# A perceiver block in one kernel: the end of attention, the first and the last group of the state-space stage in a new order

## The reference, cut to what matters

```python
x = x + xattn(layernorm(x), ctx)   # 32 query heads, 8 key/value heads of 128, RMS norm on q and k, 1601 keys
x = x + ssm(layernorm(x))          # 64 heads of 64 channels, state of 128, 8 groups
x = x + ffn(layernorm(x))          # the best of 8 experts per token, each of rank 16

# ssm, L = 64 steps:
proj = h @ in_proj.T               # gate (4096), x B C (4096 + 1024 + 1024), dt (64)
xBC  = silu(conv4(xBC) + bias)     # causal, 4 taps per channel
dt   = softplus(dt + dt_bias);  dA = exp(-exp(A_log) * dt)
state = state * dA_t + dt_t * x_t * B_t;   y_t = state @ C_t + x_t * D
y = y * rsqrt(mean(y * y over the 512 channels of a group) + eps) * norm_w * silu(gate)
out = y @ out_proj.T
```

## Time and profile before

| | us |
|---|---|
| runs | 2316.62, 2317.11, 2319.35 |
| profiled execution | 2317.6 |
| its span, from first to last instruction | 2315.2 |
| TensorE busy | 2273.6 (98%) |
| VectorE busy | 1917.5 (83%) |
| GpSimd busy | 1569.4 (68%) |
| ScalarE busy | 1300.2 (56%) |

### The profile page before, as it was taken

The page is one execution under the profiler, slowest core; times in us unless marked ns, Lnnn a source line. Parts: engine busy times, 40 slices in busy tenths (PEclk is TensorE's granted clock), DMA queues, the critical chain, the costliest instruction groups (busy, mean ns, idle before and its releaser), DMA issues. The chain is left out here.

```text
span 2315.2 us, 46570 instructions
## 1 busy us (share of the span) xinstructions
PE 2273.6 (98%) x19300; PEld 1645.4 (71%) x19300; DVE 1917.5 (83%) x2600; ACT 1300.2 (56%) x2090; POOL 1569.4 (68%) x1059
## 2 busy tenths in 40 slices
PE   8999999999999999999999999999999899999997
PEld 4577777778777778777878777877777544455554
DVE  7868888888888888888888888888888967888887
ACT  7854555545555545555545555555555446767763
POOL 0148888888888888888888788888888601433432
PEclk9999999999999999999999999999999999999999
DMA  8421000100000011000000000010001363212210
GB/s 293 128 56 35 26 19 27 29 26 27 27 27 23 29 28 33 18 27 29 27 27 27 27 22 29 27 35 10 10 29 32 112 214 110 83 65 83 92 46 19
DMA packets 101166, 117.54 MB, mean 51 GB/s; under 512 B 8286, under 2 KB 70878, under 8 KB 100958
## 3 DMA queue, kind: packets, MB, share of 16 engines
q1 hardware_dynamic: 98942, 107.25, 14.6%
q0 software_dynamic: 2016, 7.34, 1.2%
HBM read 96.74 MB, written 17.83 MB: 49 GB/s over the span
## 5 line engine op out<-in xcount | busy, mean ns | idle before, releaser
L178 POOL TENSOR_TENSOR p_l<-S,p_h 128x1792 f16<-128x1792 f32 x126 | 423.7, 3363 | 201.8 <-ACT p_h L489 201.8
L590 DVE SCALAR_TENSOR_TENSOR S<-pS,rk,mask 128x256 f32<-128x256 f32 x832 | 355.1, 477 | 130.4 <-PE pS L265 84.0
L265 PE MATMUL p_acc<-w_h,ctx_h 128*128 128x256 f16 (+1 forms) x1664 | 453.5, 273 | 2.3 <-DVE k_l L565 2.3
L265 PE MATMUL p_acc<-w_h,ctx_l 128*128 128x256 f16 (+1 forms) x1664 | 453.6, 273 | 0.0
L265 PE MATMUL p_acc<-w_l,ctx_h 128*128 128x256 f16 (+1 forms) x1664 | 453.6, 273 | 0.0
L600 DVE TENSOR_REDUCE mx<-S 128x256 f32<-128x3328 f32 x63 | 376.9, 5982 | 2.2
L265 PE MATMUL p_acc<-ctx_h,w_h 128*128 128x400 f16 x1016 | 337.6, 332 | 0.9 <-PEq L929 0.9
L265 PE MATMUL p_acc<-ctx_l,w_h 128*128 128x400 f16 x1016 | 337.6, 332 | 0.0
L471 ACT ACTIVATE v_h<-p_acc 128x512 f16<-128x512 f32 (+1 forms) x224 | 126.8, 566 | 374.2 <-PE p_acc L265 374.2
L265 PE MATMUL p_acc<-ctx_h,w_l 128*128 128x400 f16 x1016 | 336.9, 332 | 0.0
L637 DVE TENSOR_TENSOR S<-S,pO 128x1792 f32<-128x1792 f32 (+1 forms) x128 | 240.8, 1882 | 86.2 <-PE pO L335 86.2
(11 more groups left out here) (303 smaller groups left out, 5210.7 us busy)
## 6 DMA issues: line engine op xcount, KB each, us to landing
ctx_p<-ctxT_dram SPq DMA_DIRECT2D x42, 458.0 KB, 3.5
s_wst<-winG_dram SPq DMA_DIRECT2D x8, 1536.0 KB, 7.2
q_wst<-wqT_dram SPq DMA_DIRECT2D x8, 1024.0 KB, 6.4
o_scratch<-o_st SPq DMA_DIRECT2D x32, 256.0 KB, 2.4
s_wst<-winG_dram SPq DMA_DIRECT2D x8, 1024.0 KB, 5.3
m_wost<-woutG_dram SPq DMA_DIRECT2D x8, 1024.0 KB, 5.3
qh<-q_hi_scratch SPq DMA_DIRECT2D x64, 64.0 KB, 1.9
ql<-q_lo_scratch SPq DMA_DIRECT2D x64, 64.0 KB, 2.0
```

What stands on the lines that cost most here:

```text
L178: eng.tensor_tensor(p_l[:, s % 2, t0:t1, :], S[:, s % 2, t0:t1, :], p_h[:, s % 2, t0:t1, :], ALU.subtract).then_inc(pl_ok, 1)
L265: mm = pe.matmul(out, x, y, start=first and j == 0, stop=final and j == 2)
L590: ins = dve.scalar_tensor_tensor(out=S[:, s % 2, t, :].rearrange("p (r q) -> p r q", r=REP), in0=bank[:, t % 2, :].rearrange("p (r q) -> p ...
```

## The change

1. *Last unit of attention.* VectorE no longer folds: `first_maxima` is one reduce over key tiles 0 to 7, put after `output` and evacuation 5, with its output in the free half of bank `pO[1]`; `last_maxima` is a reduce over tiles 8 to 12 after evacuation 6 and a join. The tiles of projection step 1 are spread around the turns. Unit 62's sums over key tiles are no longer made by GpSimd's `total`; TensorE makes them from `p_h` and `p_l` with 26 products on ones. Step 2's low parts move from VectorE to GpSimd (ScalarE scales the stage for it); `high(4)` comes before the exponentials, `low(4)` before the last low parts.
2. *Banks of chunks.* From group 1 on, chunk n goes to `pI[(n + 1) % 3]`; output tile 1 goes to `pI[2]`. Group 1's chunks 0, 1, 2 each wait for the taps of group 0's chunks 7, 8, 9.
3. *Start.* Group 0's first `decay` comes after chunk 6, not 5. ScalarE gets a one-element Silu (`gate_table`) after `exponentials(1, 0)` in `second`, and after `exponentials(7, 1)` in `last`.
4. *Last group.* New queues on four engines. Decays 0 and 1 stand before chunks 5 and 6; the output tiles of group 6 come after all chunks, two of them in halves; the four key products lie side by side in `pI[0]`; each output tile has a bank that is free by then; `split_C` is in two parts on VectorE.

```diff
+        def in_bank(g, n):
+            return pI[(n + min(g, 1)) % 3]
         def keys_bank(g, t):
-            return pO[:, t * P:(t + 1) * P] if g == 0 else pCB
+            return pO[:, t * P:(t + 1) * P] if g == 0 else pI[0][:, t * P:(t + 1) * P] if g == L else pCB
+        def sum_bank(g, t):
+            if g == L:
+                return (pI[1], pO, pI[2], pI[0])[t]
+            return pI[2] if t == 1 or g == L - 1 and t == 3 else pO
...
+            def direct_denominators(s):
+                for t in range(KT):
+                    for part in (p_h, p_l):
+                        mm = pe.matmul(pO[s % 2][:, 1, :], ones_h[:, :], part[:, s % 2, t, :],
+                                       start=t == 0 and part is p_h, stop=t == KT - 1 and part is p_l)
+                mm.then_inc(den_ok, 1)
...
 # TensorE, last unit of attention and after it
+                        out_proj.multiply(pe, 1, (0,))
                         turn_maxima(b, s)
-                        out_proj.multiply(pe, 1, (0,))
+                        out_proj.multiply(pe, 1, (1,))
                     spread_maxima(b, s)
...
-            out_proj.multiply(pe, 1, (1, 2, 3))
-            denominators(NB - 1, U - 2)
+            direct_denominators(U - 2)
+            out_proj.multiply(pe, 1, (2, 3))
             out_proj.multiply(pe, 2, range(TT))
             for h in range(2):
                 values(NB - 1, U - 1, h)
-            out_proj.multiply(pe, 3, (0, 1))
-            denominators(NB - 1, U - 1)
-            out_proj.multiply(pe, 3, (2, 3))
+            out_proj.multiply(pe, 3, (0,))
+            denominators(NB - 1, U - 1, 1)
+            out_proj.multiply(pe, 3, (1, 2, 3))
 # VectorE, the same
             def first_maxima(s):
+                dve.wait_ge(o_ok, 2 * (U * NB - 2))
+                dve.wait_ge(s_out, 7 * (U * NB - 1) + 4)
+                dve.tensor_reduce(pO[s % 2][:, 0, :], S[:, s % 2, 0:8, :].rearrange("p t q -> p q t"), AX.X, ALU.max).then_inc(folded, 1)
+            def last_maxima(s):
...
+                dve.tensor_reduce(rest, S[:, s % 2, 8:KT, :].rearrange("p t q -> p q t"), AX.X, ALU.max).then_inc(folded, 1)
+                dve.wait_ge(folded, 2)
+                dve.tensor_tensor(mx[:, :], pO[s % 2][:, 0, :], rest, ALU.max).then_inc(mx_ok, 1)
...
             subtract(NB - 1, U - 1, 1)
-            output(NB - 1, U - 2)
-            dve.wait_ge(sum_ok, 5 * (U * NB - 1))
-            for h in range(2):
-                low(dve, NB - 1, U - 1, h)
-            total(dve, NB - 1, U - 1)
-            output(NB - 1, U - 1)
             dve.wait_ge(out_proj.lo, 8)
             out_proj.low(dve, 4)
+            low(dve, NB - 1, U - 1, 0)
+            output(NB - 1, U - 2)
+            low(dve, NB - 1, U - 1, 1)
+            total(dve, NB - 1, U - 1, 1)
+            output(NB - 1, U - 1)
...
 # input_chunk: waits
                 if n == 0:
                     wait(pe, wB_lo, g + 1)
-                    wait(pe, conv, CONV * g)
+                if n < 3:
+                    wait(pe, conv, CONV * g + (n - 2 if g == 1 else 0))
...
+            def gate_table():
+                act.activation(warm[:, :], eps[:, 0:1], ACT.Silu)
...
 # TensorE, last(g): from chunk 4 on
                 input_chunk(g, 4)
+                decay(g, 0)
                 outputs(g - 1, 3)
                 input_chunk(g, 5)
+                decay(g, 1)
+                for n in range(6, NIN):
+                    input_chunk(g, n)
+                squares(g - 1, 2)
+                squares(g - 1, 3)
+                turn_x(g, 0)
                 out_tile(g - 1, 1 - par, 0)
+                turn_x(g, 1)
+                out_tile(g - 1, 1 - par, 1, (0, 1))
+                for t in range(TT):
+                    keys_by_queries(g, t)
+                out_tile(g - 1, 1 - par, 1, (2, 3))
+                decay(g, 2)
+                outputs(g, 0)
+                out_tile(g - 1, 1 - par, 2)
+                turn_x(g, 2)
+                outputs(g, 1)
+                out_tile(g - 1, 1 - par, 3, (0, 1))
+                decay(g, 3)
+                out_tile(g - 1, 1 - par, 3, (2, 3))
+                turn_x(g, 3)
+                outputs(g, 2)
+                squares(g, 0)
+                out_tile(g, par, 0)
+                outputs(g, 3)
+                squares(g, 1)
+                out_tile(g, par, 1)
+                squares(g, 2)
+                out_tile(g, par, 2)
                 turn_normed(0)
                 squares(g, 3)
+                out_tile(g, par, 3)
                 logits(0)
-                out_tile(g, par, 3, out_bank[3])
 # VectorE, last(g): from taps 4 on
                 mean_square(g - 1)
+                times_dt(g, 0)
+                taps(g, 5)
                 accumulate(g - 1, 0)
+                times_dt(g, 1)
+                split_C(g, par, (0, 1))
+                causal(g, 0); causal(g, 1); masked(g, 0); masked(g, 1)
+                accumulate(g - 1, 1)
+                causal(g, 2); causal(g, 3); skip_added(g, 0); gated(g, par, 0); masked(g, 2)
+                accumulate(g - 1, 2)
+                times_dt(g, 2); skip_added(g, 1); gated(g, par, 1)
+                split_C(g, par, (2, 3))
+                masked(g, 3); times_dt(g, 3)
+                accumulate(g - 1, 3)
+                skip_added(g, 2); gated(g, par, 2); tile_mean_square(g, 0)
+                skip_added(g, 3); gated(g, par, 3)
                 accumulate(g, 0)
```

More of the change, by code:

```diff
@@ L550, in _ @@
             high(NB - 1, U - 1, 1)
-            for g in (4, 5, 6):
+            for g in (5, 6):
                 out_proj.high(act, g)
@@ L704, in body @@
                     evacuate(b, s, 3)
-                    if not ahead:
-                        first_maxima(s)
                     if before(b, s, 2):
@@ L723, in body @@
                     overall(b, s)
-                    if not ahead:
-                        out_proj.low_weights(dve, 2)
                     if s < NP and not last:
@@ L783, in body @@
                     squares(3)
-                    if earlier:
+                    if earlier and ahead:
                         total(pool, *earlier)
             loop(pool, body)
+            out_proj.low_of_scaled(pool, 2)
             out_proj.low_of_scaled(pool, 3)
@@ L1784, in outputs @@
                 wait(pe, yev, n)
-                wait(pe, cm, begun["cb"] if g else 0)
+                wait(pe, cm, begun["cb"] if 0 < g < L else 0)
                 wait(pe, msn, begun["ms"])
@@ L2145, in second @@
                 exponentials(1, 0)
+                gate_table()
                 finish_conv(1, 0)
@@ L2211, in last @@
                 first_tap(g, 0)
+                exponentials(g, 0)
                 square(g - 1, 3)
                 first_tap(g, 1)
+                exponentials(g, 1)
+                gate_table()
                 finish_conv(g, 0)
+                first_tap(g, 2)
                 high(g - 1, 3)
-                first_tap(g, 2)
                 finish_conv(g, 1)
@@ L2222, in last @@
                 first_tap(g, 5)
-                exponentials(g, 0)
                 finish_conv(g, 4)
+                split_C(g, par)
                 finish_conv(g, 5)
-                exponentials(g, 1)
+                exponentials(g, 2)
+                high(g, 0)
                 square(g, 0)
-                split_C(g, par)
-                high(g, 0)
-                exponentials(g, 2)
                 exponentials(g, 3)
@@ L2344, in causal @@
                 n = TT * g + t
-                wait(dve, cb, n + 1 if g else TT)
+                wait(dve, cb, n + 1 if 0 < g < L else TT * (g + 1))
                 wait(dve, m_ok, n - 1)
```

174 lines of the change are left out of this document (70 added, 104 removed).

## The result

Six runs of the changed kernel took 2301.75 to 2306.26 us, median **2304.4**; six of the kernel before on the same chip 2316.62 to 2323.05, median 2318.2. The ratio is 0.9933, 95% interval 0.9921 to 0.9944: 13.8 us faster by the medians, where 18.3 were forecast. The time lies in the range, 5.4 us above the forecast of 2299. The profiled execution took 2305.3 us, its span 2303.3.

The account below looks back on a forecast made before the run. TensorE was taken to bound nearly everything, with savings only in its idle time and low clock. Attention 4.6, state-space start 5.2 and last group 8.5 sum to 18.3 us off 2317.6 or the median 2317.11: 2299 us, range 2294 to 2309.

Parts of the forecast that it names:

- Attention: End of attention: TensorE's wait for the maxima goes, and the next block starts earlier, 4.6 us saved.
- By element: Attention's two reduces on VectorE: price goes by elements read, 3.7 us for 8 tiles and 2.3 for 5.
- Rival (2): Attention: reduce costs by output, or GpSimd's low_of_scaled slows VectorE; saves -1.3 to 1, 2304.5 to 2306 us; chance 0.10.
- Start of the state-space stage: Start of the state-space stage: turned chunk banks and an early Silu table load together save 5.2 us.
- The table: Group 1's convolution: ScalarE's Silu table load moves into a time of waiting, 0.97 us saved.
- The bank: Group 1's first chunk goes to a free bank, without waiting for the last taps; chunk (1, 0) ends 4.3 us earlier.
- Rival (3): State-space start: the waits are not removed, since silu of the same chunks comes in; 2303 us; chance 0.05.
- Last group: Last group: new order removes TensorE's waits for exponentials and GpSimd's ramp, 8.5 us saved.
- New waits: 0.8 for that mean square, 0.1 for the last squares: Last group: the only new TensorE waits in the new order, 0.8 and 0.1 us.
- Rival (1): Last group: VectorE becomes the bound, masks and skips come late, 3 us saved instead of 8.5; 2304.5 us; chance 0.20.
- sign of being wrong: Last group: a VectorE release (cbm, E, mean square) ending TensorE waits of over 3 us would show the prediction wrong.
- Rival (4): TensorE's clock: remaining pauses hold half clock, dense work behind takes double; 45 us group gives 2344 us; chance 0.04.

Follow-up runs that it names:

- Moving one call: The changed kernel with squares(7, 0) put behind out_tile(7, 0) instead of ahead of it: 2301.7 us, ratio 0.992.
- half-tile version: The changed kernel with squares(7, 0) between the halves of out_tile(7, 0), squares(7, 1) behind out_tile(7, 1), and VectorE reordered: 2299.2 us, ratio 0.9911.

## Why the prediction was right or wrong

- **What bounds the kernel**: right. The bodies kept their length to 0.01 us, and the gains are TensorE's idle time and the half clock behind it.
- **Attention, 4.6 forecast, 5.55 measured** (5.6 alone). By element was right for the reduces, 3.7 and 2.3 forecast, 3.82 and 2.46 measured; the waits on mx went. 0.7 of the missing 0.95 is the wait before the last denominators: 1.2 forecast, 0.52 measured. The block's end came as walked (0.33 of wait, 0.4 in the walk, 2.33 before). Beside a working GpSimd the reduces cost 1.87 and 1.92 ns an element, against 1.80 in the earlier trace rows (5981 ns for 3328). That is near what the Trainium skill says (SBUF — State Buffer, "Who interferes with whom"), that tensor_reduce does not contend with GpSimd on trn2; but no run has these reduces beside an idle GpSimd. The 4 and 7% may be a fixed part of each instruction: 0.26 us and 1.72 ns an element, an estimate from the reduces of 3328 and 1280 elements, give 3.78 us for 2048, and 3.82 was measured. Rival (2) fell: with PSUM or SBUF as the output the price is the same. (Its times don't follow from its condition: -1.3 to 1 in place of 4.6 gives 2302.6 to 2304.9, not 2304.5 to 2306.)
- **Start of the state-space stage, 5.2 forecast, 5.20 measured.** The two terms were tested apart. The table is worth 1.03 (0.97 forecast). The bank is worth 5.5, of which the late decay takes back 1.3; the 4.3 was the balance, and 4.2 came. Rival (3) fell.
- **Last group, 8.5 forecast, 4.0 measured.** The step that failed is the line "New waits: 0.8 for that mean square, 0.1 for the last squares". The walk let squares(7, 0) run when its squares were joined, and left out its second semaphore, `yev`, that is, skip_added(7, 2). The walk had that at 2279.5 and yet let the tile behind squares(7, 0) end at 2280.0, so start at about 2277.2. It measured 2.91 + 1.29 us of waits at `squares`, and 1.6 to 1.7 us of half clock behind the first. Moving one call gave 3.7 of the 4.5 back, and the half-tile version 5.0. The trace of the kernel before had shown the same kind of wait once, 1.29 us at squares(7, 1) for skip_added(7, 3), which the prediction doesn't name and which came again unchanged.
- **Rival (1), VectorE becomes the bound**, gave 2304.5, the time that was measured, and the prediction's sign of being wrong, that "a VectorE release (cbm, E, mean square) ends TensorE waits of over 3 us", nearly came true (2.91). As a mechanism the rival was wrong, and that its time fits is luck: the release was late for an instruction that could have stood elsewhere. It was right in part for what came next: with both squares moved, and with outputs(7, 3) ahead, the wait taken away came back on the chain over VectorE; the half-tile version got out of that.
- **The clock.** Rival (4) did not come, but the prediction's price for the clock counted only pauses it had seen. A wait of 2.9 us newly made by the change brought back 1.7 us of half clock.
- **Sum**: 5.55 + 5.20 + 4.0 = 14.75 less by stages, 13.8 by the medians; the difference is well within the start-up's spread of 6 us.

## What to carry to other kernels

When an order is written out by hand, walk it with every semaphore that an instruction waits for, also those that only keep a shared bank free, and look at what stands behind each waiting instruction: here one small product held back a finished tile. A wait of 2 to 4 us can cost more than its length, because the clock may fall behind it (1.6 us behind the 2.91 here), so the last cheap filler belongs ahead of the longest wait. After each wait taken away look for the next chain: here squares(7, 0) waited when it stood early, and when it stood late the chain behind it ended last.

## What the runs showed of the hardware

- Half clock behind a pause of TensorE is partly chance. Behind the 3.25 to 3.73 us at chunk (1, 0) the products ran at 0.43 us instead of 0.22 in all five profiles with that wait. Behind the 2.91 us at squares(7, 0) they did so in five of six. Behind the 2.31 us near 150 us it was four of fourteen, and behind the 2.16 us at turn_x(7, 0) one of three: in both profiles of the kernel before the tile behind took 2.75 us, in that of the attention part alone 3.91 us, with the same code and the same pause:

```profile
2260.58 1.09 PE L1798 MATMUL m_ab<-s_ident,m_xq 128*128 128x128 f32 x4 [2.16 <-ACT m_Ec L2072]
2261.46 0.63 PE L806 MATMUL p_acc<-m_woh,m_yh 128*128 128x512 f16 x1
```

```profile
2264.53 0.63 PE L1803 MATMUL m_ab<-s_ident,m_xq 128*128 128x128 f32 x4 [2.16 <-ACT m_Ec L2077]
2264.99 0.38 PE L811 MATMUL p_acc<-m_woh,m_yh 128*128 128x512 f16 x1
```

  The second is the second profile of the kernel before. Such episodes are part of the spread between executions of one kernel: the two at the start-up cost up to 2.9 and 1.6 us in the profiles here, where the whole spread of that stretch is 6.2.
- The length of one pause does not decide it. In the kernel before, in both its profiles, nine products ran slow behind pauses of 0.58, 1.39 and 0.81 us within 5 us (the third low stretch of the earlier trace rows), and at the start-up slow products came behind pauses of 1.65 and 1.74 us in two profiles, with 9 us of idle not long ahead, and not behind 1.67 and 1.72 in two others; behind single pauses of 1.65, 2.00 and 2.11 us in the last group none did.
- The fall can come after the pause is over, up to 1.4 us in these profiles: in the changed kernel TensorE resumed at 2272.02 and started four products of the tile 0.22 us apart before the slow ones began, at 2273.1.
